# Dense turn on one Trainium2 core: the last two value products ahead of the fourth projection, the second pair of turned rows ahead of a score product, half a narrowing ahead of two transposes

## The reference, cut to what matters

```
q, k, v = xn @ Wq + bq, xn @ Wk + bk, xn @ Wv + bv      # 8 heads of 32, windows of 64 keys each side
p = softmax(mask(q k^T * 32**-0.5));  o = p v;  attn = o @ Wo + bo
x2 = layernorm(xn + attn) * gamma + beta
block = x2 + gelu(x2 @ W1 + b1) @ W2 + b2                # W1: 256 -> 1024, W2: 1024 -> 256
experts: top 2 of 8, each silu((x gp^T + b) * (x up^T + b)) @ down^T + b, 816 wide
```

## Time and profile before

| | |
|---|---|
| median of 3 runs | 1162.81 us |
| the profiled execution | 1163.15 us, its span 1161.3 us, mean granted TensorE clock 0.974 |
| TensorE matmul busy | 1051.1 us (91%) |
| TensorE weight load busy | 961.3 us (83%) |
| ScalarE busy | 836.9 us (72%) |
| VectorE busy | 822.6 us (71%) |
| GpSimd busy | 739.2 us (64%) |

### The profile page before, as it was taken

One profiled execution on the slowest core, in us unless ns is written; L12 is line 12 of the kernel. 1 busy time (PEld: TensorE's weight loads), 2 busy tenths in 40 slices (PEclk: granted clock), 3 DMA queues, 4 the chain that ended last, 5 costly groups with the idle time before them and its releaser, 6 DMA issues.

```text
span 1161.3 us, 29369 instructions
## 1 busy us (share of the span) xinstructions
PE 1051.1 (91%) x8776; PEld 961.3 (83%) x8776; DVE 822.6 (71%) x1930; ACT 836.9 (72%) x1988; POOL 739.2 (64%) x1037
## 2 busy tenths in 40 slices
PE   1778999999999999979899999999999999999994
PEld 1556878787878787868899999999999999999994
DVE  5277566666666666665888888888888887888871
ACT  4565858686868676754887777777777887777882
POOL 5335737272726363622577888877788888887775
PEclk8789999999999999989999999999999999999998
DMA  9791012020202010411621222235521253125510
GB/s 314 250 304 36 28 53 70 25 68 27 68 27 68 27 45 28 167 34 64 231 59 29 32 36 36 36 89 164 177 60 29 34 169 75 30 36 153 158 47 2
DMA packets 62772, 98.36 MB, mean 85 GB/s; under 512 B 9424, under 2 KB 52432, under 8 KB 61072
## 3 DMA queue, kind: packets, MB, share of 16 engines
q1 hardware_dynamic: 47648, 78.16, 21.3%
q0 software_dynamic: 15088, 19.75, 9.0%
HBM read 130.13 MB, written 37.50 MB: 144 GB/s over the span
## 4 chain that ended last, share of the span: by engine, by line
PE 29%; ACT 21%; DVE 21%; issue 18%; POOL 5%; DMA 3%; DVEq 1%; POOLq 0%; ACTq 0%; SPq 0%
PE bank L1263 6%; DVE gu_s L1190 6%; PE bank L1265 6%; PE bank L1264 6%; ACT sm L742 4%; DVE gu_s L1183 4%; ACT hf L843 4%; DVE sm L1036 3%; PE bank L1366 3%; PE bank L1394 3%; PE bank L1356 2%; POOL ht L634 2%; DVE ys L1219 2%; DVE hf L1203 2%; DMA out_dram<-ys,dest 2%
## 5 line engine op out<-in xcount | busy, mean ns | idle before, releaser
L1263 PE MATMUL bank<-xt_h,gu_s 128*128 128x256 f32 (+1 forms) x1014 | 290.6, 287 | 4.8 <-DVE hf L1203 2.5
L1264 PE MATMUL bank<-xt_l,gu_s 128*128 128x256 f32 (+1 forms) x1014 | 287.6, 284 | 0.0
L1265 PE MATMUL bank<-xt_h,gu_s 128*128 128x256 f32 (+1 forms) x1014 | 287.1, 283 | 0.0
L634 POOL TENSOR_TENSOR ht<-hf,ht 128x256 fp32r<-128x256 f32 (+1 forms) x273 | 228.8, 840 | 90.7 <-ACT ht L847 79.6
L1190 DVE TENSOR_TENSOR gu_s<-raw_gu,gu_s 128x512 fp32r<-128x512 f32 (+1 forms) x273 | 193.6, 731 | 64.0 <-ACT gu_s L854 63.9
L1263 PEld LDWEIGHTS bank<-xt_h,gu_s 128*128 128x128 f32 (+1 forms) x1014 | 192.6, 190 | 5.5 <-DVE xt_l L1211 2.8
L1265 PEld LDWEIGHTS bank<-xt_h,gu_s 128*128 128x128 f32 (+1 forms) x1014 | 192.3, 190 | 0.0
L1264 PEld LDWEIGHTS bank<-xt_l,gu_s 128*128 128x128 f32 (+1 forms) x1014 | 191.9, 189 | 0.0
L836 ACT ACTIVATE gs<-bank,bias 128x256 f32<-128x256 f32 x234 | 110.4, 472 | 90.8 <-PE bank L1265 87.0
L646 POOL DMA_INDIRECT out_dram<-ys,dest x78 | 127.8, 1638 | 54.4 <-POOL ht L634 30.7
L1263 PE MATMUL bank<-dw_s,ht 128*128 128x256 f32 x468 | 135.8, 290 | 17.4 <-POOL dw_s L625 15.5
(11 more groups left out here) (182 smaller groups left out, 2668.1 us busy)
## 6 DMA issues: line engine op xcount, KB each, us to landing
raw_gu<-in_gu_dram SPq DMA_DIRECT2D x39, 1648.0 KB
raw_dw<-in_dw_dram SPq DMA_DIRECT2D x39, 768.0 KB
xs_dram<-zrec SPq DMA_DIRECT2D x6, 1677.0 KB, 18.2
xr<-xs_dram SPq DMA_DIRECT2D x39, 258.0 KB, 2.9
xwin<-xt_dram SPq DMA_DIRECT2D x8, 640.0 KB
raw_dw<-in_dw_dram SPq DMA_DIRECT2D x78, 64.0 KB
xg<-in_x_dram SPq DMA_DIRECT2D x8, 512.0 KB, 7.1
xt_dram<-xt SPq DMA_DIRECT2D x8, 512.0 KB, 3.6
```

The lines of the kernel that those rows point to most:

```text
L634: nc.gpsimd.tensor_tensor(low, hf[0:m, ring(c), :], ht[0:m, p, 0, c, :].bitcast(F32), ALU.subtract).then_inc(h_split, 1)
L1263: nc.tensor.matmul(dst, lhs[0], rhs[0], start=start, stop=False)
L1264: nc.tensor.matmul(dst, lhs[0], rhs[1], start=False, stop=False)
L1265: return nc.tensor.matmul(dst, lhs[1], rhs[0], start=False, stop=stop)
```

## The change

TensorE's order in a turn changes in three places: the products V3 and V4 both stand ahead of `out_project(3)`, where V4 stood behind it; `turn_x2(at, 1)` stands ahead of `scores(at, GT + 1)`; and chunks 0 to 3 of the narrowing of tile 1 stand ahead of `half_slot(0)`. V3 and V4 leave the shared banks for the two banks of the transposes (V3 in `t_bank[1]`, V4 in `t_bank[0]`), and the counts on these banks' semaphores get one more for each turn but the closing one. In the shared banks A3 and Y3 change places in the alternation: A3 is now in the bank of V2 and X0, Y3 in the bank of O3 and X1. The order on ScalarE and VectorE stays; ScalarE's two copies wait on the other semaphores.

```
 TURN = (["Y0", "Y1", "O0", "A0", "Y2", "O1", "A1", "Q0", "Q1", "K0", "O2", "K1", "V1",
-         "A2", "V2", "O3", "V3", "A3", "V4", "Y3", "X0", "X1"] + [f"F{c}" for c in range(FC1)])
+         "A2", "V2", "O3", "A3", "Y3", "X0", "X1"] + [f"F{c}" for c in range(FC1)])
+def t_count(bank, tile, uses, turn):
+    return tile * (3 - bank) + uses + (turn.g if turn.seg != "first" else 0)
+def late_value(turn, j):
+    bank = GT - j
+    return bank, t_count(bank, turn.g * GT + GT, 1, turn)
...
# ScalarE: v_copy(at, 3) and v_copy(at, 4) become v_late
+            def v_late(at, j):
+                b, n = late_value(at, j)
+                act.wait_ge(t_full[b], n)
+                nc.scalar.activation(v[:, j, :, :], t_bank[b][:, 0:D].rearrange("p (h d) -> p h d", d=DH), ACT.Copy).then_inc(t_free[b], 1)
...
# TensorE
+            def values_late(at, j):
+                b, n = late_value(at, j)
+                pe.wait_ge(t_free[b], n)
+                for k in range(KC):
+                    ins = passes(t_bank[b][:, 0:D], pair(xw_h, xw_l, every, k, slice(j * P, (j + 1) * P)), parts(wv_s, k, every), k == 0, k == KC - 1)
+                ins.then_inc(t_full[b], 1)
...
                 begin_slot(0)
                 fill(0, *range(FC1))
+                fill(1, 0, 1, 2, 3)
                 half_slot(0)
-                fill(1, *range(FC1))
+                fill(1, 4, 5, 6, 7)
                 turn_shares(at, 0)
...
                 times_v(at, 3)
                 if more:
-                    values(at, 3)
+                    values_late(at, 3)
+                    values_late(at, 4)
                 out_project(at, 3)
-                if more:
-                    values(at, 4)
                 fill(3, *range(FC1))
                 turn_x2(at, 0)
+                turn_x2(at, 1)
                 if more:
                     scores(at, GT + 1)
-                turn_x2(at, 1)
```

More of the change, by code:

```diff
@@ L452, in _ @@
             turn(Turn("mid", NG - 2, NG - 3))
-            b, n = m_use("V4", Turn("mid", NG - 2, NG - 3))
-            sp.wait_ge(m_full[b], n + 1)
+            b, n = late_value(Turn("mid", NG - 2, NG - 3), GT)
+            sp.wait_ge(t_full[b], n)
             sp.wait_ge(slots_ready, 1)
@@ L743, in probs, with pt_copy, shares_copy @@
                                          accum_out=total[:, j % 2, c, r:r + 1]).then_inc(probs_ready, 1)
-            def pt_copy(g, j, r):
-                n = g * GT + j
-                act.wait_ge(t_full[r % 2], n * 3 + 2 if r == 2 else n * 2 + (r // 2 + 1))
+            def pt_copy(at, j, r):
+                act.wait_ge(t_full[r % 2], t_count(r % 2, at.g * GT + j, r // 2 + 1, at))
                 nc.scalar.activation(pt[:, r].rearrange("p a n -> p (a n)"), t_bank[r % 2][:, :], ACT.Copy).then_inc(t_free[r % 2], 1)
-            def shares_copy(g, j):
-                n = g * GT + j
-                act.wait_ge(t_full[0], n * 3 + 3)
+            def shares_copy(at, j):
+                act.wait_ge(t_full[0], t_count(0, at.g * GT + j, 3, at))
                 nc.scalar.activation(shares[:, j % 2, :], t_bank[0][:, 0:D], ACT.Copy).then_inc(t_free[0], 1)
@@ L782, in turn @@
                 for j in range(GT):
-                    pt_copy(g, j, 1)
+                    pt_copy(at, j, 1)
                     if j == 0:
@@ L790, in turn @@
                         v_copy(at, 2)
-                    pt_copy(g, j, 2)
+                    pt_copy(at, j, 2)
                     if more and j == 2:
@@ L795, in turn @@
                         probs(at, j + 1, 1 if j else 0)
-                    pt_copy(g, j, 3)
+                    pt_copy(at, j, 3)
                     if more and j == 2:
@@ L803, in turn @@
                         probs(at, j + 1, 3)
-                    shares_copy(g, j)
+                    shares_copy(at, j)
                     if more and j == 2:
@@ L809, in turn @@
                         probs(at, GT, 0)
-                        v_copy(at, 3)
+                        v_late(at, 3)
                         probs(at, GT, 1)
@@ L818, in turn @@
                     act.wait_ge(v_kept, g + 1)
-                    v_copy(at, 4)
+                    v_late(at, 4)
                 act.wait_ge(ln_stats, g * GT + GT)
@@ L1046, in share_of, with pt_copy @@
                                       spread(share[:, j % 2].rearrange("p c r -> p (c r)"), [P, H, DH])).then_inc(share_ready, 1)
-            def pt_copy(g, j):
-                dve.wait_ge(t_full[0], (g * GT + j) * 3 + 1)
+            def pt_copy(at, j):
+                dve.wait_ge(t_full[0], t_count(0, at.g * GT + j, 1, at))
                 nc.vector.tensor_copy(pt[:, 0].rearrange("p a n -> p (a n)"), t_bank[0][:, :]).then_inc(t_free[0], 1)
@@ L1054, in normalise @@
                 bk, free = full(f"O{j}", at)
-                dve.wait_ge(t_free[0], n * 3 + 4)
+                dve.wait_ge(t_free[0], t_count(0, n, 4, at))
                 nc.vector.tensor_tensor(ot[:, :, :].rearrange("p k n -> p (k n)"), bk[:, 0:D], shares[:, j % 2, :], ALU.mult).then_inc(free, 1)
@@ L1115, in turn @@
                     mask = end if at.seg == "last" and j == GT - 2 else mid
-                    pt_copy(g, j)
+                    pt_copy(at, j)
                     if j == 0 and at.seg != "first":
@@ L1362, in turn_probs @@
                 pe.wait_ge(probs_ready, n * H + (2 * r + 2))
-                pe.wait_ge(t_free[r % 2], n * 2 + (r // 2 + 1) if r % 2 else n * 3 + (r // 2 + 1))
+                pe.wait_ge(t_free[r % 2], t_count(r % 2, n, r // 2 + 1, at))
                 for c in range(KC):
@@ L1372, in turn_shares @@
                 pe.wait_ge(share_ready, n + 1)
-                pe.wait_ge(t_free[0], n * 3 + 3)
+                pe.wait_ge(t_free[0], t_count(0, n, 3, at))
                 for c in range(KC):
@@ L1381, in times_v @@
                 bk, full = take(f"O{j}", at)
-                pe.wait_ge(t_free[0], n * 3 + 3)
-                pe.wait_ge(t_free[1], n * 2 + 3)
+                pe.wait_ge(t_free[0], t_count(0, n, 3, at))
+                pe.wait_ge(t_free[1], t_count(1, n, 3, at))
                 for c in range(KC):
```

## The result

The kernel after takes 1154.11 us (median of 7 runs, 1150.81 to 1158.32) against 1162.82 us before; the ratio is 0.9926, 95% interval 0.9909 to 0.9944. The forecast was 1154.0 us. The profiled execution after took 1153.56 us with a span of 1151.7 us.

What follows compares the result with a forecast made beforehand. TensorE was taken to bound the dense part, idle 3.8 us of a 58.5 us middle turn. 6 x (1.15 + 0.2) + 0.5 + 0.2 = 8.8 us off 1162.8 gave 1154.0 us, range 1150 to 1159.5.

Steps and rivals of the forecast that it cites:

- Part 1: Middle turn's end: V4 (0.90 us) fills the 1.04 us gap ahead of the fourth projection, which keeps its place.
- The layer norm 1.0 us earlier: Middle turn's end: V4's earlier copy and table load let the layer norm start at 228.6 instead of 229.66.
- Part 2: X1 ahead of the scores waits for Y3's sum; the widening's 0.62 us gap goes; 1.15 us a turn with V4's move.
- Part 3: Slot 0: half a narrowing (1.45 us) ahead of pair 2; ScalarE's chain slips 0.45 us, so only 0.2 us a turn gained.
- The opening turn: Gain of 0.5 us (0 to 1.2), as other VectorE work holds the layer norm there.
- phase against TensorE stays: GpSimd's work hangs on the sum of Y3, which comes about 1.1 us earlier, nearly as much as the turn.
- the six middle turns look alike: Reading of the profile before: TensorE's gaps at the places of the change are alike in all six middle turns.
- All gaps at slot 0 come out: Rival: ScalarE has reserve at slot 0, 7 x 0.9 us more, 15.1 in all, 1147.7 us; chance 0.06.
- The layer norm hardly moves: Rival: 2.66 us between V4's copy and the root, 0.4 us a turn, 1158.5 us; chance 0.15, shared with a slot 0 loss.
- slower, by the clock: Rival: the wait ahead of X1 drops TensorE's clock in each middle turn, 1169 us; chance 0.06, shared with another loss.

Runs made afterwards that it cites:

- part 1 alone: Kernel after with the old order of X1 and scores and the whole narrowing in its old place: 57.54 us a middle turn, 1156.15 us, ratio 0.9945.
- the early copy of the shares: Kernel after with ScalarE's copy of the shares ahead of the next tile's exponentials of pairs 2 and 3, slots 0 to 2: 1146.21 us, ratio 0.9853.
- two chunks: Kernel after with two instead of four chunks of tile 1's narrowing ahead of pair 2's transposes: 56.85 us a middle turn, 1154.51 us, ratio 0.9923.
- eight: Kernel after with all eight chunks of tile 1's narrowing ahead of pair 2's transposes: 58.63 us a middle turn, 1162.67 us, ratio 0.9994.
- four pieces: Kernel after with GpSimd's window subtraction in four pieces of 144 columns instead of one: 1152.29 us, ratio 0.9907.
- the short subtraction: Kernel after with GpSimd's subtraction in the first middle turn over 32 of 576 columns only: 1152.41 us, ratio 0.9902.
- part 2 alone: Kernel before with X1 ahead of the scores, V3 and V4 as before: 58.53 us a middle turn, 1162.11 us, ratio 0.9999.

## Why the prediction was right, step by step

- **Part 1, right.** The projection kept its place with 0.32 us of idle time ahead (0.3 forecast); X0 came 3.80 us behind it (forecast 4.0).
- **The layer norm 1.0 us earlier, right.** It moved by 1.08 us. The load ended at 225.20 and the root ran at 225.69, on its own wait for the statistics; 0.49 us behind the load is less than the 1.38 us of draining that the Trainium skill names (ScalarE: Activation LUTs, "What ACT_TABLE_LOAD costs"). From the end of V4's copy (223.90) to the root are 1.79 us in all, not 2.66. The measurement decides against the rival built on it.
- **Part 2: the sum right, the step wrong in its share.** I forecast 1.15 us for both parts and 1.11 came. But I wrote that the gap of 0.62 us "goes" by X1's new place, and that would have been a gain of part 2. The runs show part 1 gives 0.99 alone and part 2 0.02. In the old order X1 comes right behind the scores, and the second half waits for X1's rests; in the new one X1 waits and the scores come later. Both paths end at 8.3 us; that they end together follows from nothing that the prediction worked out, and it did not see it. My 0.8 for part 1 alone missed that the scores, too, start earlier there: X1 stood 5.45 us behind the projection, not 5.7.
- **Part 3: the mechanism right, the size a little low.** 0.27 us against 0.2. Pair 2 came 0.44 us later (forecast 0.54), ScalarE's copy of it 0.33 us later (forecast 0.45; 247.09 less 241.35 against 5.41 before), the copy of the shares 0.34, and slot 1 started 0.3 us earlier.
- **The opening turn, mis-sized.** 0.5 forecast (0 to 1.2), 1.97 in the profiled execution. An estimate from the granted clock: TensorE worked at 1.2 GHz for about 6.2 us there before and 3.1 us after, and half of the difference, 1.5 us, is the clock's part (below).
- **The first middle turn, a step that failed.** I wrote that GpSimd's "phase against TensorE stays". This holds where its work hangs on the sum of Y3. In the first middle turn it hangs on the scattering of the first group, which does not move when the opening turn ends earlier. The 17.1 us that the earlier trace rows give as the longest wait belong to the later turns; here GpSimd waited 2.02 us, for the scattering, and "the six middle turns look alike" did not hold for it. The copy on VectorE then falls into the long subtraction: 2.96 us lost in the profiled execution. That the total came out as forecast is partly chance: against the forecast the opening turn gave 1.5 us more, the first middle turn 3.2 us less (-2.96 against 0.2), and 1.9 us at the start and 0.8 us at the end came that the forecast did not have. The five intervals behind it, 6.7 us, are the part that was worked out and held.
- **The rivals.** "All gaps at slot 0 come out" was wrong for this kernel, and the early copy of the shares shows what it wanted. "The layer norm hardly moves" and "slower, by the clock" did not occur: the middle turns stay at clock 1.00.

## What to carry to other kernels

Fill an engine's gap no further than the gap is long when another engine's chain starts behind it: two chunks gave twice what four gave, and eight cost the whole gain of the change. Before work is moved, look for the one short instruction of the other engine that frees a buffer, here a copy of 0.36 us that stood behind four exponentials that the next slot did not need; moving it forward was worth nearly as much as the whole change. And where two wait chains end within 0.1 us of each other, a gap seen on one of them is not a gain.

## What the runs showed of the hardware

**VectorE's copy behind GpSimd.** In ten traces the copy that met the long subtraction ended 0.14 to 0.16 us behind its end, whether it had begun 0.1 us (2.64 us long) or 2.2 us (0.60) behind its start. With four pieces it ended 0.15 us behind the piece that ran when it began: behind the second in one trace (140.33 against 140.18), behind the first in the other (143.44 against 143.29). The minimum and mask instructions on VectorE, which read PSUM, took 0.41 to 0.42 us each beside GpSimd and alone. The Trainium skill (SBUF — State Buffer, section "Who interferes with whom") says that a VectorE copy can enter a mode that uses two ports, one pair of which it shares with GpSimd, and that then the first to issue has the shared pair for its whole instruction while the other is fully blocked. The times agree; which mode this copy ran in no row shows. The runs add that cutting the GpSimd instruction is enough to let the copy in.

**The clock in the opening turn.** Nearly the same work behind 3.1 to 3.7 us of idle time ran at 1.2 GHz (0.50) for very different times. Stretches before, after and, in the third fence, with the short subtraction, columns as in the earlier trace rows:

```profile
110.00:112.00 2.00, 0.97 (x4) 0.68 (x4) 1.93 (x5) 0.00 (x0) 1.31 (x4) 0.60 0.19 66
...
114.00:116.00 2.00, 2.00 (x13) 1.94 (x10) 0.09 (x1) 0.77 (x2) 0.65 (x3) 0.50 0.01 4
```

```profile
110.00:112.00 2.00, 2.00 (x20) 1.46 (x18) 1.23 (x2) 1.65 (x3) 0.98 (x1) 0.54 0.00 0
112.00:114.00 2.00, 2.00 (x21) 1.73 (x14) 0.15 (x1) 0.66 (x1) 0.38 (x2) 1.00 0.19 66
```

```profile
112.00:114.00 2.00, 2.00 (x16) 1.32 (x9) 0.51 (x1) 1.02 (x1) 0.64 (x3) 0.50 0.07 25
114.00:116.00 2.00, 2.00 (x12) 1.96 (x11) 0.00 (x0) 0.15 (x1) 1.18 (x3) 0.62 0.00 0
```

With part 2 alone TensorE idled 3.08 us there and the clock stayed at 1.00.

The way from the opening turn's projection to the next turn took 18.7 to 19.5 us in nine profiled executions with the new order of X1 and 21.1 in a tenth, the short subtraction's, whose TensorE program is the same as after's; part 2 may still give something there, as the old order took 20.1 to 21.5 in three. How much of that is order and how much chance of the clock was not told apart.
